# Experts' second product: high and low weight parts as one 512-column moving operand, its halves summed at the end of a block

## The chip, the cores and the metric

One core of a Trainium2 chip. The metric is the device time of one execution in microseconds (us), the median of several runs.

## The reference

A sequence of two layers over x of 2 x 2048 tokens and width D = 256: relative-position attention, then a pre-norm layer with plain attention and a mixture of experts. Only the experts concern the change:

```
h = layernorm(x, ln2_g, ln2_b).reshape(B * S, D)
topv, topi = top_k(h @ gate_w + gate_b, 2)
ew = sum(one_hot(topi, 8) * softmax(topv)[..., None], axis=1)
hid = relu(einsum('td,edf->etf', h, W1) + b1[:, None, :])      # DFF = 1024
out_e = einsum('etf,efd->etd', hid, W2) + b2[:, None, :]
moe = einsum('etd,te->td', out_e, ew)
```

The kernel computes only the two chosen experts of each token.

## The kernel before

The attentions and the routing fill the first 3790 us. Routing writes the tokens' rows, sorted by expert, to `sorted_rows`; `expert_stage` then works through NBLK = 39 blocks of BT = 256 rows, each for one expert. A block's 256 rows are BJ = 2 halves of 128, its 1024 hidden columns are FC = 8 chunks of 128. A unit u is one chunk of one block: b = u // 8, f = u % 8. There are 312 units.

Products keep their precision by parts: each operand is split into a high part and a low part (the rest) of the type fp32r, and three of the four products are taken: `PARTS = ((0, 0), (0, 1), (1, 0))`, index 0 for high and 1 for low.

The engines run side by side, each with its own program in a fixed order, tied by semaphores:

- SyncE's queue loads per block the rows xb, the first weight r1 (L2332, 1 MB), the second weight w2, already split in an earlier stage (L2336, 2 MB, three buffers; it waits for s_s, TensorE's last use of the buffer three blocks back), and b2.
- TensorE per unit, in this order: `first(u + 2)` (L2382, six matmuls of 256 columns into psH), `second(u)` (L2396, six matmuls of 256 columns, three per half j, accumulated into psY over the block's 8 units), and after the unit with f = 1 `turn(b + 1)` (L2368, four transposes of the next block's rows into psT). `second(u)` first waits for s_lo, the low part of the hidden values of unit u. Each matmul has a weight load (LDWEIGHTS, shown as PEld) of its own.
- ScalarE per unit: two activations of psH, to `whole` and to the high part `hid[:, 0]` (L2432). For f = 2 and 3 also one copy of psT to hb (L2418), which waits for `turn`, and for f = 5 and 6 yb, the bias times the row's weight (L2440).
- VectorE per unit: the low part `hid[:, 1]` (L2508), which waits for ScalarE's activations (s_r) and raises s_lo. Behind it, by f: for 0 to 2 and 7 the parts of the next first weight (L2451, L2456); for f = 3 `finish(b - 1)` (L2496), which reads the previous block's psY; for f = 4 `split_h(b + 1)` (L2464, L2466); for f = 5 `pick(b + 1)`.
- GpSimd per block: two scatter-adds of y to the output (L2353).

psY is [128, 2, BJ, 512] of fp32 in PSUM: one bank of 512 columns for each parity q of the block and each half j; before the change only 256 of the 512 columns are used.

Of the kernel before, what the change touches and what calls it, by code (L numbers as in the profile page):

```python
# [9 lines left out]
ALU = mybir.AluOpType  # L10
AX = mybir.AxisListType

P = 128
D = 256
# [10 lines left out]
FC = DFF // P  # L25
# [101 lines left out]
NP2 = 2  # L127
# [1705 lines left out]
BJ = BT // P  # L1833
# [8 lines left out]
PARTS = ((0, 0), (0, 1), (1, 0))  # L1842
# [427 lines left out]
def expert_stage(nc, A, xs, w2_parts, acc, ident, gain, b1_t, onehot, tab):  # L2270
# [8 lines left out]
    NHID = 4  # L2279
    NW2 = 3  # L2280
    NID = 4
    with ExitStack() as ctx:  # L2282
        def sb(name, shape, dt=F32):
            return ctx.enter_context(nc.sbuf_tensor("mo_" + name, shape, dt))
# [3 lines left out]
        def sem(name):  # L2288
            sems.append(ctx.enter_context(nc.semaphore("mo_" + name)))
            return sems[-1]  # L2290

        r1 = sb("w1_raw", [P, 2, CH, DFF])
        w1, w2 = sb("w1_parts", [P, 2, 2, CH, DFF], F32R), sb("w2_parts", [P, NW2, NP2, FC, D], F32R)
# [5 lines left out]
        hid = sb("hid_parts", [P, 2, NHID, BT], F32R)  # L2299
        wsel, b1sel = sb("wsel", [P, 2, BJ, NE]), sb("b1sel", [P, 2, FC, NE])  # L2300
        wt, b1 = sb("wt", [P, 2, BJ]), sb("b1", [P, 2, FC])
        ids = sb("ids", [P, NID, BJ], U32)
        yb = sb("yb", [P, 2, BJ, D])
        y = sb("y", [P, 2, BJ, D])
        psT = ctx.enter_context(nc.psum_tensor("mo_psT", [P, CH, BT], F32))
        psH = ctx.enter_context(nc.psum_tensor("mo_psH", [P, 3, G], F32))
# [6 lines left out]
        s_t, s_hT, s_hs, s_hs1 = (sem(n) for n in ("s_t", "s_hT", "s_hs", "s_hs1"))  # L2313
        s_1h, s_1l = (sem(n) for n in ("s_1h", "s_1l"))
        s_h, s_r, s_lo, s_s = (sem(n) for n in ("s_h", "s_r", "s_lo", "s_s"))
        s_pick, s_wt, s_yb, s_y = (sem(n) for n in ("s_pick", "s_wt", "s_yb", "s_y"))
        ctx.callback(clear_semaphores, nc, sems)
        blk = ctx.enter_context(nc.Block())

# [40 lines left out]
        @blk.tensor  # L2360
        def _(pe):
            def turn(b):
                pe.wait_ge(s_x[b % 3], 16 * (b // 3 + 1))
                if b >= 1:
                    pe.wait_ge(s_hT, CH * b)
                for c in range(CH):
                    for j in range(BJ):
                        last = pe.transpose(psT[:, c, j * P:(j + 1) * P], xb[:, b % 3, j, c * P:(c + 1) * P],  # L2368
                                            ident[:, :])
                last.then_inc(s_t, 1)  # L2370

            def first(u):
                b, f = u // FC, u % FC
                q = b % 2
                if f == 0:
                    pe.wait_ge(s_hs, b + 1)
                    pe.wait_ge(s_1l, CH * (b + 1))
                if u >= 3:
                    pe.wait_ge(s_r, 2 * (u - 2))
                for c in range(CH):  # L2380
                    for m, (x, z) in enumerate(PARTS):
                        last = pe.matmul(psH[:, u % 3, 0:BT], w1[:, q, x, c, f * P:(f + 1) * P], hp[:, q, z, c, :],  # L2382
                                         start=c == 0 and m == 0, stop=c == CH - 1 and m == len(PARTS) - 1)
                last.then_inc(s_h, 1)

            def second(u):
                b, f = u // FC, u % FC
                q = b % 2
                pe.wait_ge(s_lo, u + 1)
                if f == 0:  # L2390
                    pe.wait_ge(s_w2[b % NW2], 16 * (b // NW2 + 1))
                for j in range(BJ):
                    if f == 0 and b >= 2:
                        pe.wait_ge(s_y, BJ * (b - 2) + j + 1)
                    for m, (x, z) in enumerate(PARTS):
                        last = pe.matmul(psY[:, q, j, 0:D], hid[:, x, u % NHID, j * P:(j + 1) * P],  # L2396
                                         w2[:, b % NW2, z, f, :], start=f == 0 and m == 0,
                                         stop=f == FC - 1 and m == len(PARTS) - 1)
                last.then_inc(s_s, 1)

            turn(0)
            first(0)
            first(1)
            for u in range(NU):
                if u + 2 < NU:
                    first(u + 2)
                second(u)
                if u % FC == 1 and u // FC + 1 < NBLK:
                    turn(u // FC + 1)
# [33 lines left out]
        @blk.vector  # L2443
        def _(dve):
            def high_w1(b, c):
                q = b % 2
                if c == 0:
                    dve.wait_ge(s_r1[q], 16 * (b // 2 + 1))
                    if b >= 2:
                        dve.wait_ge(s_h, FC * (b - 1))  # L2450
                dve.tensor_copy(w1[:, q, 0, c, :], r1[:, q, c, :]).then_inc(s_1h, 1)  # L2451

            def low_w1(b, c):
                q = b % 2
                dve.wait_ge(s_1h, CH * b + c + 1)
                dve.tensor_tensor(out=w1[:, q, 1, c, :], in0=r1[:, q, c, :], in1=w1[:, q, 0, c, :], op=ALU.subtract  # L2456
                                  ).then_inc(s_1l, 1)

            def split_h(b):
                q = b % 2  # L2460
                dve.wait_ge(s_hT, CH * (b + 1))
                if b >= 2:
                    dve.wait_ge(s_h, FC * (b - 1))
                dve.tensor_copy(hp[:, q, 0, :, :], hb[:, q, :, :]).then_inc(s_hs1, 1)  # L2464
                dve.wait_ge(s_hs1, b + 1)
                dve.tensor_tensor(out=hp[:, q, 1, :, :], in0=hb[:, q, :, :], in1=hp[:, q, 0, :, :], op=ALU.subtract  # L2466
                                  ).then_inc(s_hs, 1)

            def pick(b):
                q = b % 2  # L2470
                dve.wait_ge(s_x[b % 3], 16 * (b // 3 + 1))
                if b >= 2:
                    dve.wait_ge(s_r, 2 * FC * (b - 1))
                    dve.wait_ge(s_yb, BJ * (b - 1))
                if b >= NID:
                    dve.wait_ge(s_sc[q], 16 * BJ * (b // 2 - 1))
                one = onehot[:, b:b + 1, :]
                dve.tensor_tensor(out=wsel[:, q, :, :], in0=xb[:, b % 3, :, EW0:EW0 + NE],
                                  in1=one.to_broadcast([P, BJ, NE]), op=ALU.mult).then_inc(s_pick, 1)
                dve.tensor_tensor(out=b1sel[:, q, :, :], in0=b1_t[:, :, :], in1=one.to_broadcast([P, FC, NE]),  # L2480
                                  op=ALU.mult).then_inc(s_pick, 1)
                dve.tensor_copy(ids[:, b % NID, :], xb[:, b % 3, :, ID0]).then_inc(s_pick, 1)
                dve.wait_ge(s_pick, 4 * b + 2)
                dve.reduce_sum(wt[:, q, :], wsel[:, q, :, :], AX.X).then_inc(s_pick, 1)
                dve.wait_ge(s_pick, 4 * b + 4)
                dve.reduce_sum(b1[:, q, :], b1sel[:, q, :, :], AX.X).then_inc(s_wt, 1)

            def finish(b):
                q = b % 2
                dve.wait_ge(s_s, FC * (b + 1))  # L2490
                dve.wait_ge(s_yb, BJ * (b + 1))
                dve.wait_ge(s_wt, b + 1)
                if b >= 2:
                    dve.wait_ge(s_sc[q], 16 * BJ * (b // 2))
                for j in range(BJ):
                    dve.scalar_tensor_tensor(out=y[:, q, j, :], in0=psY[:, q, j, 0:D], scalar=wt[:, q, j:j + 1],  # L2496
                                             in1=yb[:, q, j, :], op0=ALU.mult, op1=ALU.add).then_inc(s_y, 1)

            pick(0)
            split_h(0)  # L2500
            for c in range(CH):
                high_w1(0, c)
            for c in range(CH):
                low_w1(0, c)
            for u in range(NU):
                b, f = u // FC, u % FC
                dve.wait_ge(s_r, 2 * (u + 1))
                dve.tensor_tensor(out=hid[:, 1, u % NHID, :], in0=whole[:, u % NHID, :], in1=hid[:, 0, u % NHID, :],  # L2508
                                  op=ALU.subtract).then_inc(s_lo, 1)
                if b + 1 < NBLK:  # L2510
                    if u == 0:
                        high_w1(1, 0)
                    if f == 0:
                        low_w1(b + 1, 0)
                    if f == 1:
                        high_w1(b + 1, 1)
                    if f == 2:
                        low_w1(b + 1, 1)
                if f == 3 and b >= 1:
                    finish(b - 1)  # L2520
                if b + 1 < NBLK:
                    if f == 4:
                        split_h(b + 1)
                    if f == 5:
                        pick(b + 1)
                if f == 7 and b + 2 < NBLK:
                    high_w1(b + 2, 0)
            finish(NBLK - 1)


# [90 lines left out]
```

## Time and profile before

| | |
|---|---|
| runs, us | 4268.16, 4260.19, 4265.67 |
| median, us | 4265.67 |
| span of the profiled execution, us | 4272.5 |
| TensorE busy, us (share) | 3916.3 (92%) |
| VectorE busy, us (share) | 3446.8 (81%) |
| ScalarE busy, us (share) | 2970.6 (70%) |
| experts' stage | from about 3790 us to the end |

The span is that of one profiled execution, from its first to its last instruction; no separate time of that execution was given beside it, and it lies 6.8 us above the median of the timed runs. "PE" is TensorE's matmuls, "PEld" its weight loads, which overlap the matmuls, "DVE" VectorE, "ACT" ScalarE, "SPq" the DMA queue of SyncE. A matmul's shown duration includes its way through the pipeline, so it is longer than the distance to the next one; the distances between starts tell the pace.

### The profile page before, as it was taken

How to read it: one execution, taken by the hardware profiler on the slowest of the kernel's cores; microseconds unless marked ns; L12 is line 12 of the kernel's file. 1: busy time of each engine (PE TensorE's matmuls, PEld its weight loads, DVE VectorE, ACT ScalarE, POOL GpSimd, SP SyncE). 2: the span in 40 equal slices, each digit the busy share in tenths (PEclk: the TensorE clock that was granted, in tenths of full speed). 3: DMA queues.
4: the chain of work that ended last, by engine and by line, in shares of the span. 5: the costliest groups of instructions: out<-in, count | busy, mean ns of one | idle time of the engine just before them, and what ended most of it. 6: DMA issues, size and time to landing. Idle time of an engine off the chain costs nothing. (4 is left out here: it accounts for less than half of the span.)

```text
span 4272.5 us, 78522 instructions
## 1 busy us (share of the span) xinstructions
PE 3916.3 (92%) x26838; PEld 2067.2 (48%) x26838; DVE 3446.8 (81%) x6397; ACT 2970.6 (70%) x5963; POOL 1500.0 (35%) x1461
## 2 busy tenths in 40 slices
PE   8699999999999999996879999999999999759998
PEld 5344545545455445543533333333333333659998
DVE  7788888888888888862778889898888884657776
ACT  4077878778878777884218888888888887236666
POOL 0356666666666665652110000001010100533333
PEclk9599999999999999998969999999999999779999
DMA  8666666667677767643773333334243331679997
GB/s 315 156 162 162 163 165 168 161 163 168 163 165 168 166 161 169 167 120 108 243 155 60 64 60 64 61 56 77 47 72 56 63 53 41 160 264 325 322 326 222
DMA packets 479567, 636.81 MB, mean 149 GB/s; under 512 B 61752, under 2 KB 404520, under 8 KB 464960
## 3 DMA queue, kind: packets, MB, share of 16 engines
q1 hardware_dynamic: 460640, 608.46, 55.7%
q0 software_dynamic: 18528, 23.34, 2.9%
q8 instruction: 213, 3.49, 0.4%
q14 instruction: 186, 1.52, 0.1%
HBM read 413.78 MB, written 216.78 MB: 148 GB/s over the span
## 5 line engine op out<-in xcount | busy, mean ns | idle before, releaser
L399 DVE TENSOR_REDUCE pa_pm<-pa_psA 128x2 f32<-128x1024 f32 x1024 | 1208.3, 1219 | 133.5 <-PE pa_psA L484 133.3
L1122 ACT ACTIVATE ra_p<-ra_psS 128x512 f32<-128x512 f32 x2048 | 1082.4, 605 | 316.1 <-PE ra_psS L1199 224.2
L1033 DVE TENSOR_REDUCE ra_pm<-ra_psA 128x1 f32<-128x896 f32 x1024 | 1113.2, 1087 | 157.1 <-PE ra_psA L1157 142.2
L458 ACT ACTIVATE pa_p<-pa_psS 128x512 f32<-128x512 f32 x2048 | 1063.4, 603 | 245.9 <-PE pa_psS L510 241.7
L510 PE MATMUL pa_psS<-pa_qs,pa_zs 50*128 50x512 f32 x2048 | 792.1, 464 | 77.9 <-ACT pa_p L458 63.9
L484 PE MATMUL pa_psA<-pa_zs,pa_qs 48*128 48x512 f32 x2048 | 795.6, 471 | 38.4 <-DMA pa_zs<-k_halves 18.2
L1157 PE MATMUL ra_psA<-ra_zs,ra_qs 48*128 48x512 f32 x2048 | 730.7, 451 | 19.3 <-DVE ra_pm L1035 8.4
L1199 PE MATMUL ra_psS<-ra_qs,ra_zs 50*128 50x512 f32 (+3 forms) x2176 | 699.7, 407 | 28.9 <-ACT ra_p L1122 20.7
L510 PEld LDWEIGHTS pa_psS<-pa_qs,pa_zs 50*128 50x128 f32 x2048 | 341.6, 184 | 625.4 <-ACT pa_p L458 609.2
L1230 PE MATMUL ra_psO<-ra_p,ra_vs 128*32 128x512 f32 (+3 forms) x6400 | 552.8, 450 | 0.0
L1199 PEld LDWEIGHTS ra_psS<-ra_qs,ra_zs 50*128 50x128 f32 x2176 | 351.1, 186 | 412.1 <-ACT ra_p L1122 318.1
L521 PE MATMUL pa_psO<-pa_p,pa_vs 128*32 128x512 f32 x4096 | 546.3, 605 | 0.0
L484 PEld LDWEIGHTS pa_psA<-pa_zs,pa_qs 48*128 48x128 f32 x2048 | 346.0, 189 | 207.8 <-DVE pa_pm L399 160.0
L1157 PEld LDWEIGHTS ra_psA<-ra_zs,ra_qs 48*128 48x128 f32 x2048 | 322.6, 191 | 130.5 <-DVE ra_pm L1035 68.4
L363 POOL COPY pa_vs<-pa_vall 128x256 f32<-128x256 f32 x32 | 12.7, 398 | 1014.9 <-PE pa_psO L521 981.1
L973 POOL TENSOR_TENSOR ra_blk<-ra_blk 128x508 f32<-128x508 f32 x128 | 162.8, 1272 | 415.9 <-DMA ra_blk<-window_rows 380.1
L2382 PE MATMUL mo_psH<-mo_hp,mo_w_parts 128*128 128x256 f32 x1872 | 277.8, 285 | 5.9 <-DVE mo_w_parts L2456 5.9
L2396 PE MATMUL mo_psY<-mo_w_parts,mo_hid_parts 128*128 128x256 f32 x1872 | 273.2, 282 | 3.1 <-DVE mo_hid_parts L2508 3.1
L2353 POOL DMA_INDIRECT out<-mo_y,mo_ids x78 | 143.5, 1840 | 351.4 <-DVE mo_y L2496 331.0
L1230 PEld LDWEIGHTS ra_psO<-ra_p,ra_vs 128*32 128x32 f32 x6400 | 193.2, 109 | 121.2 <-ACT ra_p L1122 59.0
L2382 PEld LDWEIGHTS mo_psH<-mo_hp,mo_w_parts 128*128 128x128 f32 x1872 | 245.1, 190 | 6.2 <-issue 6.2
L2396 PEld LDWEIGHTS mo_psY<-mo_w_parts,mo_hid_parts 128*128 128x128 f32 x1872 | 243.6, 189 | 3.5 <-DVE mo_hid_parts L2508 3.5
(247 smaller groups left out, 4995.7 us busy)
## 6 DMA issues: line engine op xcount, KB each, us to landing
mo_w_parts<-second_weight_parts SPq DMA_DIRECT2D x39, 2048.0 KB
relative_rows<-ra_rst SPq DMA_DIRECT2D x128, 512.0 KB
ra_blk<-window_rows SPq DMA_DIRECT2D x128, 512.0 KB, 4.6
ra_zs<-k_halves SPq DMA_DIRECT2D x192, 248.0 KB, 7.6
mo_w_raw<-ffn_W SPq DMA_DIRECT2D x39, 1024.0 KB, 11.6
ra_dl<-relative_rows SPq DMA_DIRECT2D x128, 256.0 KB, 5.5
window_rows<-ra_pc SPq DMA_DIRECT2D x128, 256.0 KB, 4.4
pa_qs<-q_halves SPq DMA_DIRECT2D x192, 128.0 KB, 6.4
```

What stands on the lines that cost most here:

```text
L399: dve.reduce_max(pm[:, par, 2 * a:2 * a + 2], psA[w][:, :, :], AX.X).then_inc(s_am.h, 1)
L458: act.activation(pr[:, i % NPR, :], psS[:, slot(i), :], ACT.Exp).then_inc(s_ex.h, 1)
L484: last = pe.matmul(psA[w][:, half, :], qs[0:PR, k % U, i * P:(i + 1) * P], zs[0:PR, k % U, e * G:(e + 1) * G], start=True, stop=True)
L510: pe.matmul(psS[:, slot(i), :], zs[at:at + PR + NP2, p % U, z * P:(z + 1) * P], qs[at:at + PR + NP2, p % U, c * G:(c + 1) * G], start=True ...
L521: last = pe.matmul(psO[32 * m:32 * m + 32, :], vs[:, p % 2, 4 * (k % 4) + m, :], pr[:, (4 * k + m) % NPR, :], start=k % 4 == 0, stop=k % 4 ...
L1033: dve.reduce_max(pm[:, q, i, 2 * left:2 * left + 1], psA[w][:, lo:lo + 2 * G - P], AX.X).then_inc(s_far.h, 1)
L1122: act.activation(dst, psS[:, slot(i), :], ACT.Exp if kind == "E" else ACT.Copy).then_inc(s_cp.h, 1)
L1157: last = pe.matmul(psA[w][:, half * G:(half + 1) * G], qs[0:PR, q, i * P:(i + 1) * P], zs[0:PR, q, at:at + G], start=True, stop=True)
L1199: last = pe.matmul(dst[:, lo:hi], zs[at:at + PR + NP2, q, z * P:(z + 1) * P], qs[at:at + PR + NP2, q, c * G + lo:c * G + hi], start=True, ...
L1230: last = pe.matmul(psO[32 * m:32 * m + 32, lo:hi], v[:, z, :], pr[:, (4 * k + m) % NPR, lo:hi], start=n == 0, stop=n == 3, tile_position=( ...
L2382: last = pe.matmul(psH[:, u % 3, 0:BT], w1[:, q, x, c, f * P:(f + 1) * P], hp[:, q, z, c, :], start=c == 0 and m == 0, stop=c == CH - 1 an ...
L2396: last = pe.matmul(psY[:, q, j, 0:D], hid[:, x, u % NHID, j * P:(j + 1) * P], w2[:, b % NW2, z, f, :], start=f == 0 and m == 0, stop=f == ...
```

## The change

In `second`, the matmul of the high hidden part with the high part of the weight and the one with the low part become one: the moving operand is both parts, 2 x 256 = 512 columns, and the output is the whole bank of psY, the first 256 columns for the high part and the other 256 for the low part. The third matmul (low hidden part, high weight part) adds into the first 256 columns as before. In `finish`, the two halves are summed: a first operation per j computes yc = psY[256:512] x wt + yb, and a second y = psY[0:256] x wt + yc, which waits for the first through the new semaphore s_yc. yc is a new buffer in SBUF.

```
-        yb = sb("yb", [P, 2, BJ, D])
+        yb, yc = sb("yb", [P, 2, BJ, D]), sb("yc", [P, 2, BJ, D])
...
-                    for m, (x, z) in enumerate(PARTS):
-                        last = pe.matmul(psY[:, q, j, 0:D], hid[:, x, u % NHID, j * P:(j + 1) * P],
-                                         w2[:, b % NW2, z, f, :], start=f == 0 and m == 0,
-                                         stop=f == FC - 1 and m == len(PARTS) - 1)
+                    pe.matmul(psY[:, q, j, :].rearrange("p (z d) -> p z d", z=NP2), hid[:, 0, u % NHID, j * P:(j + 1) * P],
+                              w2[:, b % NW2, :, f, :], start=f == 0, stop=False, skip_group_check=True)
+                    last = pe.matmul(psY[:, q, j, 0:D], hid[:, 1, u % NHID, j * P:(j + 1) * P], w2[:, b % NW2, 0, f, :],
+                                     start=False, stop=f == FC - 1, skip_group_check=True)
                 last.then_inc(s_s, 1)
...
                 for j in range(BJ):
+                    dve.scalar_tensor_tensor(out=yc[:, q, j, :], in0=psY[:, q, j, D:2 * D], scalar=wt[:, q, j:j + 1],
+                                             in1=yb[:, q, j, :], op0=ALU.mult, op1=ALU.add).then_inc(s_yc, 1)
+                for j in range(BJ):
+                    dve.wait_ge(s_yc, BJ * b + j + 1)
                     dve.scalar_tensor_tensor(out=y[:, q, j, :], in0=psY[:, q, j, 0:D], scalar=wt[:, q, j:j + 1],
-                                             in1=yb[:, q, j, :], op0=ALU.mult, op1=ALU.add).then_inc(s_y, 1)
+                                             in1=yc[:, q, j, :], op0=ALU.mult, op1=ALU.add).then_inc(s_y, 1)
```

## Rows read from the trace of the kernel before

**Rows 1.** The page: the span.

```profile
span 4272.5 us, 78522 instructions
```

**Rows 2.** Busy time by stretch, instructions (x), granted clock, DMA share, GB/s.

```profile
3300.00:3400.00 100.00, 93.62 (x610) 31.61 (x608) 89.77 (x84) 81.14 (x158) 9.05 (x7) 1.00 0.35 60
...
3700.00:3800.00 100.00, 52.46 (x243) 47.06 (x243) 46.46 (x235) 20.27 (x32) 50.09 (x50) 0.61 0.62 190
...
4000.00:4100.00 100.00, 100.00 (x850) 100.00 (x849) 77.13 (x176) 67.82 (x166) 30.57 (x17) 1.00 0.96 326
```

**Rows 3.** Waits from 3800 us on: total us, times, longest.

```profile
POOL out L2353 <- DVE mo_y L2496: 331.0, 38, 49.4
...
PEld mo_psY L2396 <- DVE mo_hid_parts L2508: 3.5, 2, 3.3
...
SPq L2336 <- PE mo_psY L2396: 287.5, 36, 8.9
```

**Rows 4.** The chain that ended last: start us, us, what.

```profile
3840.27 0.72 PE mo_psH L2382 x6
...
4241.69 0.72 PE mo_psH L2382 x6
```

**Rows 5.** Timeline of the weight loads in one block: start us, us, what.

```profile
4004.85 0.47 PEld L2368 LDWEIGHTS mo_psT<-ident,mo_xb 128*128 128x128 f32 x4
...
4006.00 0.78 PEld L2396 LDWEIGHTS mo_psY<-mo_w_parts,mo_hid_parts 128*128 128x128 f32 x6
4006.71 0.78 PEld L2382 LDWEIGHTS mo_psH<-mo_hp,mo_w_parts 128*128 128x128 f32 x6
...
4008.84 0.78 PEld L2396 LDWEIGHTS mo_psY<-mo_w_parts,mo_hid_parts 128*128 128x128 f32 x6
...
4010.26 0.78 PEld L2396 LDWEIGHTS mo_psY<-mo_w_parts,mo_hid_parts 128*128 128x128 f32 x6
```

**Rows 6.** Timeline of VectorE in the same block.

```profile
4006.92 0.43 DVE L2508 TENSOR_TENSOR mo_hid_parts<-mo_hid,mo_hid_parts 128x256 fp32r<-128x256 f32 x1 [1.46 <-ACT mo_hid_parts L2432]
4007.27 0.87 DVE L2496 SCALAR_TENSOR_TENSOR mo_y<-mo_psY,mo_wt,mo_yb 128x256 f32<-128x256 f32 x2
4008.11 0.43 DVE L2508 TENSOR_TENSOR mo_hid_parts<-mo_hid,mo_hid_parts 128x256 fp32r<-128x256 f32 x1
4008.45 0.42 DVE L2464 CAST mo_hp<-mo_hb 128x512 fp32r<-128x512 f32 x1
4008.91 0.69 DVE L2466 TENSOR_TENSOR mo_hp<-mo_hb,mo_hp 128x512 fp32r<-128x512 f32 x1
4009.52 0.42 DVE L2508 TENSOR_TENSOR mo_hid_parts<-mo_hid,mo_hid_parts 128x256 fp32r<-128x256 f32 x1
...
4010.53 0.41 DVE L2508 TENSOR_TENSOR mo_hid_parts<-mo_hid,mo_hid_parts 128x256 fp32r<-128x256 f32 x1
```

**Rows 7.** Timeline of ScalarE in the same block.

```profile
4005.59 0.57 ACT L2418 ACTIVATE mo_hb<-mo_psT,gain 128x256 f32<-128x256 f32 x1 [1.73 <-PE mo_psT L2368]
...
4006.42 0.48 ACT L2432 ACTIVATE mo_hid_parts<-mo_psH,mo_b 128x256 fp32r<-128x256 f32 x1
```

**Rows 8.** Timeline of TensorE in the plain attention, 512 columns.

```profile
2503.09 0.40 PE L510 MATMUL pa_psS<-pa_qs,pa_zs 50*128 50x512 f32 x1
2503.09 0.40 PE L484 MATMUL pa_psA<-pa_zs,pa_qs 48*128 48x512 f32 x1
2503.32 0.41 PE L510 MATMUL pa_psS<-pa_qs,pa_zs 50*128 50x512 f32 x1
2503.33 0.41 PE L484 MATMUL pa_psA<-pa_zs,pa_qs 48*128 48x512 f32 x1
```

**Rows 9.** Groups by line: count, busy us, mean ns, idle before.

```profile
L2496 DVE SCALAR_TENSOR_TENSOR mo_y<-mo_psY,mo_wt,mo_yb 128x256 f32<-128x256 f32 x78 | 34.0, 477 | 1.2 <-PE mo_psY L2396 1.1
```

**Rows 10.** Timeline of the last units and the last `finish`.

```profile
4258.94 0.43 DVE L2508 TENSOR_TENSOR mo_hid_parts<-mo_hid,mo_hid_parts 128x256 fp32r<-128x256 f32 x1 [0.99 <-ACT mo_hid_parts L2432]
4259.42 0.77 PEld L2396 LDWEIGHTS mo_psY<-mo_w_parts,mo_hid_parts 128*128 128x128 f32 x6 [0.18 <-DVE mo_hid_parts L2508]
4260.43 0.88 DVE L2496 SCALAR_TENSOR_TENSOR mo_y<-mo_psY,mo_wt,mo_yb 128x256 f32<-128x256 f32 x2 [1.06 <-PE mo_psY L2396]
```

More of the change, by code:

```diff
@@ L2315, in expert_stage @@
         s_h, s_r, s_lo, s_s = (sem(n) for n in ("s_h", "s_r", "s_lo", "s_s"))
-        s_pick, s_wt, s_yb, s_y = (sem(n) for n in ("s_pick", "s_wt", "s_yb", "s_y"))
+        s_pick, s_wt, s_yb, s_yc, s_y = (sem(n) for n in ("s_pick", "s_wt", "s_yb", "s_yc", "s_y"))
         ctx.callback(clear_semaphores, nc, sems)
```

## The prediction

> **What bounds the kernel now.** I read the page first: the profiled execution spans 4272.5 us [rows 1], 6.8 us (0.16%) more than the median of the timed runs, 4265.67. The sum below is made against that span, and its difference is carried over to the median. Then the table of stretches [rows 2]: the experts' stage, where the whole change lies, runs from about 3790 us on, and there TensorE's busy time, weight loads' busy time and the DMA share are 100, 100 and 96 of 100, at a granted clock of 1.00, which is 2.4 GHz. Two candidates for the bound, so the waits decide [rows 3]: TensorE waited for VectorE 3.5 us in the whole stage and for no DMA, while the DMA queue that loads the second weights sat 287.5 us waiting for TensorE to be done with a buffer. So the order is: TensorE sets the pace, the DMA queue is paced by it, and the DMA engines have about 4% in hand. The chain that ended last says the same [rows 4]: from 3840.27 to 4241.69 it is 34 equal blocks, 401.42 / 34 = 11.806 us each.
>
> Inside a block I read the weight loads in order of time [rows 5]. Six pairs of load and matmul of the second product start at 4006.00 and the next six at 4006.71, so a pair costs 118 ns; 256 columns at 2.4 GHz are 107 ns of it. VectorE in the same stretch [rows 6] is where the little slack is. The low part for f = 3 (L2508) starts at 4006.92, then `finish` runs its two operations, then the low part for f = 4 runs 4008.11 to 4008.54, and TensorE takes it at 4008.84. What anchors this is not the matmuls of the last few units but the four transposes of `turn` at 4004.85: ScalarE's hb follows them, then its copies for f = 3, which end at 4006.90 [rows 7], and VectorE's low part starts 0.02 later.
>
> **What the change removes on TensorE.** One matmul and one weight load of each three, 624 of each over 39 blocks x 8 units x 2 halves. The columns streamed stay 768 per unit and half, so only what a pair costs beyond its columns can be saved. Before, three pairs are 3 x 118 = 354 ns. After, one pair of 512 columns and one of 256. The trace has no 128-row matmul of 512 columns of this type at full clock with a load before each; the nearest are the attention's [rows 8], where two matmuls of 512 columns follow at 2503.09 and 2503.33 (0.23 to 0.24 us apart on the two lines). By that row: 235 + 118 = 353, a saving of 1 ns, and -4 at the upper reading. By the pair's own fixed part (118 - 107 = 11 ns, the same at any width): 224 + 118 = 342, a saving of 12. If the wide pair had no fixed part at all it would be 213 + 118 = 331, a saving of 23, the bound below. I take 6 ns, between the two likelier ends: 16 per block x 6 = 0.10 us per block, 3.7 us over the stage if nothing else happened.
>
> The Trainium skill has a rule here (TensorE: Matmul & The Clock Gate, Back-to-back issue gap): isolated matmuls are spaced by their columns over 2.4 GHz plus about 2.5 ns, so three of 256 would be about 328 ns and 512 + 256 about 325. By that rule the saving would be 3 ns, inside the bounds above; the trace's 118 ns for 256 columns with a load before each [rows 5] is more than the rule's 109, so I work from the rows.
>
> **What it adds on VectorE.** Two more operations of 128x256 in each `finish`, 78 in all. The existing two take 0.87 us from start to end and one alone is 477 ns on average [rows 6, 9], so the second starts 0.87 - 0.48 = 0.39 after the first. The new wait of the first y on s_yc is for an operation that ended about 0.3 us before, since another lies between; I cost it at nothing, and at most 0.05 each. So `finish` grows by 2 x 0.39 = 0.79 us, at most 0.9. VectorE as a whole has room (77 of 100 busy [rows 2], and 0.79 / 11.8 adds 7), but `finish` is placed ahead of the low part for f = 4, for which TensorE waits.
>
> The step: the low part for f = 4 now starts at 4008.11 + 0.79 = 4008.90 and ends at 4009.33. From its end to the load that waits for it the trace shows 0.05 us (4258.94 + 0.43 to 4259.42, the one late wait of [rows 10]). The load can start at 4009.38; it would have started at 4008.84. TensorE stands 0.54 us. Behind it everything on TensorE moves by that much, since it issues in order: `first` of f = 7, the next weights' release. What is late next? On VectorE, split_h and the low part for f = 5 move by 0.79 too: from 4009.52 to 4010.31, end 4010.73, plus 0.05 is 4010.78; TensorE comes for it at 4010.26 + 0.54 = 4010.80. So it is just in time, and the later ones gain room (f = 6 starts 1.0 us after f = 5, TensorE asks 1.42 after). ScalarE isn't late: it waits for TensorE's first product, which is issued two units ahead. By the end of the block VectorE has caught up, TensorE can't, and as VectorE's place in the next block hangs on `turn`, which moved with TensorE, the stall comes back in each block.
>
> Per block: + 0.54, less the saving. Of the 16 savings, the four between `turn` and the stall (f = 2 and 3) buy nothing, since the stall's end is set by VectorE: TensorE only arrives earlier. 12 x 6 ns = 0.07. Net + 0.47 us per block. It needs a `finish` before f = 4 and a `turn` before it: blocks 1 to 37, so 37 x 0.47 = 17.4. Blocks 0 and 38 save 0.2 together. In block 38 there is no turn and ScalarE has less to do, so its low parts come earlier and I count no stall.
>
> **The end.** The last `finish` waits for the last matmul and its two operations start at 4260.43 [rows 10]; the scatters follow. The first y is written 0.79 us later: + 0.8.
>
> **The DMA side** gets easier: the same bytes per block in 12.3 instead of 11.8 us. The scatter-add's engine waited 331 us for y [rows 3], so y's 0.79 us delay lies beside idle time, apart from the end. yc costs memory only. PSUM: the 512-column write fills the bank that `finish` does not read in that block.
>
> Sum: 17.4 - 0.2 + 0.8 = + 18.0 us. The profile's span would be 4290.5, the median 4283.7.
>
> **Rivals.**
> 1. *The added VectorE work stays hidden* (not slower). It decides at 0.25 us: if the two operations delay the low part for f = 4 by less than that (0.30 of slack less 0.05 of signalling), TensorE never stands. For it: VectorE has 23% idle. Against: that idle time lies elsewhere, the low part before `finish` had idle time ahead of it because of ScalarE [rows 6], and none lies between `finish` and f = 4. Time: - 3.7 + 0.8 = - 2.9, 4263; with the largest saving (23 ns x 624 = 14.4) 4252.
> 2. *A wide matmul costs far less than two narrow ones* (faster). If weight loads and not columns set the pace, 512 columns cost like 256: 118 ns saved per unit and half, 12 x 0.118 = 1.42 per block against 0.54. Then the DMA engines would be the bound: at a share of 0.96 [rows 2] the block can shrink by 4%, 0.47 us, so 37 x 0.47 = 17.4 us less and 0.8 more at the end, 4249. Against: the attention's wide matmuls are 0.23 us apart [rows 8], and TensorE's transposes with half the columns take 109 ns (4 loads in 0.47, the last one 0.14 [rows 5]), less than the 118.
> The Trainium skill would have it so: the same section of the same page gives a sustained 131 ns for a matmul of 512 columns with its load. The rows of the attention do not bear that out.
> 3. *The stall is larger*: with 0.45 per operation and a costly s_yc wait, 0.9 + 0.1 instead of 0.79, f = 5 late by a further few hundredths, and no saving at all: 0.75 per block, + 28.6, 4294.
> 4. *The pauses lower the clock.* In 3700 to 3800 the granted clock is 0.61 with TensorE 52 of 100 busy; in 3300 to 3400 it is 1.00 with 94 busy [rows 2]. After the change TensorE is idle 0.54 of 12.3 us, 4%. At 94 busy it stayed up, so I give this 2%; a tenth of the stage at half clock would be + 44, 4328.
>
> **Chances.** Forecast (a net loss of 0.25 to 0.65 per block) 0.78; rival 1 0.10; rival 2 0.03; rival 3 0.07; rival 4 0.02. The forecast's own bounds: stall 0.54 with the full 23 ns gives 37 x (0.54 - 0.28) = 9.6 - 0.7 + 0.8 = + 9.7, 4275; 0.9 of added work with no saving, 37 x 0.65 + 0.8 = + 25, 4291. Range 4272 to 4293. About 0.2% (8.5 us) is what a measurement here can tell from no change: slower by more than that is the forecast nearly whole and rivals 3 and 4, 0.84; within 0.2% most of rival 1, and a forecast at its lower end, 0.11; faster, rival 2 and rival 1 with the large saving, 0.05.
>
> **What would show it.** In the changed profile: a new wait of the L2396 load for L2508, some 37 times, each about 0.54, 20 us in total, always the unit after `finish`; four operations in `finish` in 1.65 us; blocks of 12.28 us in the chain; 512-column matmuls 224 to 235 ns before the next start; DMA share down to about 0.93. I am wrong if that wait is missing or shorter than 0.2 us, if the block is 11.8 or less, or if a unit other than f = 4 stalls.

## The result and the profile after

The changed kernel takes 4281.49 us, median of 13 runs (4269.62 to 4293.79), beside 4268.26 us for the kernel before in its 13 runs on the same chips (4260.19 to 4278.5). The ratio is 1.0036, 95% interval 1.0025 to 1.0047: slower by 0.36%, some 15 us (the two medians alone are 13.2 apart), where +18.0 us (0.42%) was forecast.

The page of the changed kernel, span and busy time:

```profile
span 4281.9 us, 77353 instructions
...
PE 3922.3 (92%) x26214; PEld 2037.9 (48%) x26214; DVE 3479.9 (81%) x6475; ACT 2968.8 (69%) x5963; POOL 1492.5 (35%) x1461
```

Its waits from 3800 us on (who waited for whom: total us, times, longest us), and the DMA queue's own:

```profile
POOL out L2353 <- DVE mo_y L2500: 349.5, 38, 48.3
...
PEld mo_psY L2395 <- DVE mo_hid_parts L2512: 16.0, 38, 0.4
PE mo_psY L2395 <- DVE mo_hid_parts L2512: 8.3, 37, 0.2
...
SPq L2336 <- PE mo_psY L2397: 302.2, 36, 8.8
```

Against [rows 3], one wait is new: the weight load of the second product waits for the low part of the hidden values in every block, where the whole stage of before had 3.5 us of it. The view counts only idle time of the engine (a load shown as 0.19 us overlaps the next), so 0.4 here isn't the whole delay. That is read from the timeline of one block, the weight loads first (start us, us, what):

```profile
4005.34 0.47 PEld L2368 LDWEIGHTS mo_psT<-ident,mo_xb 128*128 128x128 f32 x4
...
4007.90 0.19 PEld L2395 LDWEIGHTS mo_psY<-mo_w_parts,mo_hid_parts 128*128 128x128 f32 x1
...
4009.80 0.19 PEld L2395 LDWEIGHTS mo_psY<-mo_w_parts,mo_hid_parts 128*128 128x128 f32 x1 [0.43 <-DVE mo_hid_parts L2512]
```

and VectorE in the same block:

```profile
4007.42 0.42 DVE L2512 TENSOR_TENSOR mo_hid_parts<-mo_hid,mo_hid_parts 128x256 fp32r<-128x256 f32 x1 [1.43 <-ACT mo_hid_parts L2432]
...
4007.76 0.87 DVE L2496 SCALAR_TENSOR_TENSOR mo_yc<-mo_psY,mo_wt,mo_yb 128x256 f32<-128x256 f32 x2
...
4008.55 0.87 DVE L2500 SCALAR_TENSOR_TENSOR mo_y<-mo_psY,mo_wt,mo_yc 128x256 f32<-128x256 f32 x2
...
4009.33 0.42 DVE L2512 TENSOR_TENSOR mo_hid_parts<-mo_hid,mo_hid_parts 128x256 fp32r<-128x256 f32 x1
```

`finish` occupies 4007.76 to 4009.33, 1.57 us for four operations (0.39 each). The low part for f = 4 ends at 4009.75, and the load that needs it starts at 4009.80. From the first transpose of `turn` to that load it is now 4009.80 - 4005.34 = 4.46 us; before it was 4008.84 - 4004.85 = 3.99 [rows 5]. The low part for f = 3, anchored to `turn` through ScalarE, has kept its place: 2.08 us after it, 2.07 before [rows 5, 6].

The length of a block is the distance of `turn` from block to block. The first transpose loads of two blocks that lie 33 apart, changed kernel:

```profile
3834.70 0.37 PEld L2368 LDWEIGHTS mo_psT<-ident,mo_xb 128*128 128x128 f32 x3
...
4236.93 0.37 PEld L2368 LDWEIGHTS mo_psT<-ident,mo_xb 128*128 128x128 f32 x3
```

402.23 / 33 = 12.189 us, against 11.806 [rows 4]: +0.383 per block. TensorE's matmuls in the changed kernel, in order of time:

```profile
4001.95 0.39 PE L2395 MATMUL mo_psY<-mo_w_parts,mo_hid_parts 128*128 128x512 f32 x1
...
4002.18 0.28 PE L2397 MATMUL mo_psY<-mo_w_parts,mo_hid_parts 128*128 128x256 f32 x1
...
4002.30 0.39 PE L2395 MATMUL mo_psY<-mo_w_parts,mo_hid_parts 128*128 128x512 f32 x1
...
4002.52 0.28 PE L2397 MATMUL mo_psY<-mo_w_parts,mo_hid_parts 128*128 128x256 f32 x1
...
4002.64 0.88 PE L2382 MATMUL mo_psH<-mo_hp,mo_w_parts 128*128 128x256 f32 x6
```

Wide to narrow 0.22 to 0.23 us, narrow to the next 0.12: 0.345 us for both at this place, where three narrow ones took 0.354. So the removed work did give time back, and the stall took more. The stretch 4000 to 4100 shows the stall as well: matmuls 98.23 of 100, where they were 100 before, VectorE 81.50, and the clock still 1.00. Weight loads are at 91.22, in part because there are fewer of them:

```profile
4000.00:4100.00 100.00, 98.23 (x691) 91.22 (x691) 81.50 (x188) 66.39 (x164) 29.91 (x17) 1.00 0.96 317
```

From the first transpose of the stage to the end, the changed kernel takes 4281.9 - 3780.03 = 501.9 us; its row is

```profile
3780.03 0.50 PEld L2368 LDWEIGHTS mo_psT<-ident,mo_xb 128*128 128x128 f32 x3 [27.68 <-DMA mo_xb<-sorted_rows]
```

and the kernel before

```profile
3785.29 0.50 PEld L2368 LDWEIGHTS mo_psT<-ident,mo_xb 128*128 128x128 f32 x3 [26.88 <-DMA mo_xb<-sorted_rows]
```

so 4272.5 - 3785.3 = 487.2 us. The stage grew by 14.7 us. The two spans differ by only 9.4, because the stage happened to begin 5.3 us sooner, with nothing changed ahead of it. The stage's own length leaves that out, and I use it and the block's length beside the ratios below. The stage has some scatter of its own at its start: from its first transpose to the `turn` of the third block it took 30.65 us before and 30.29 in the changed kernel, 30.3 to 30.7 in nine of the ten traces of this document, and 27.84 in the tenth (that of the last experiment). The block's length is the steadiest of the three.

### The profile page after: what moved, and what is told of

It reads as the page before. It is cut to its first block and busy times, and to the rows that moved or that the text cites. A ratio compares the mean times of both kernels' runs of the same rounds, so it can differ in the third digit from the quotient of the medians.

```text
span 4281.9 us, 77353 instructions
## 1 busy us (share of the span) xinstructions
PE 3922.3 (92%) x26214; PEld 2037.9 (48%) x26214; DVE 3479.9 (81%) x6475; ACT 2968.8 (69%) x5963; POOL 1492.5 (35%) x1461
## 5 line engine op out<-in xcount | busy, mean ns | idle before, releaser
L484 PE MATMUL pa_psA<-pa_zs,pa_qs 48*128 48x512 f32 x2048 | 795.9, 471 | 38.3 <-DMA pa_zs<-k_halves 18.2
L2395 PE MATMUL mo_psY<-mo_w_parts,mo_hid_parts 128*128 128x512 f32 x624 | 235.0, 398 | 11.7 <-DVE mo_hid_parts L2512 11.7
L1128 ACT ACTIVATE ra_sw<-ra_sw,ra_nm 128x256 f32<-128x256 f32 x512 | 243.6, 529 | 0.0
```

The source lines that it names most:

```text
L484: last = pe.matmul(psA[w][:, half, :], qs[0:PR, k % U, i * P:(i + 1) * P], zs[0:PR, k % U, e * G:(e + 1) * G], start=True, stop=True)
L2395: pe.matmul(psY[:, q, j, :].rearrange("p (z d) -> p z d", z=NP2), hid[:, 0, u % NHID, j * P:(j + 1) * P], w2[:, b % NW2, :, f, :], start=f ...
```

## The experiments

The first four ran together on one chip, the last four on another; each group is compared with runs of the kernel before on the same chip (medians 4262.59 and 4273.69 us). Of the account to be tested, two parts can be separated: longer VectorE work in `finish`, and the wide matmul.

**VectorE's part alone.** Six narrow matmuls as before; in `finish`:

```
+                for j in range(BJ):
+                    dve.scalar_tensor_tensor(out=yc[:, q, j, :], in0=psY[:, q, j, 0:D], scalar=wt[:, q, j:j + 1],
+                                             in1=yb[:, q, j, :], op0=ALU.mult, op1=ALU.add).then_inc(s_yc, 1)
                 for j in range(BJ):
+                    dve.wait_ge(s_yc, BJ * b + j + 1)
                     (y as before)
```

> VectorE's part alone: the kernel before with its six narrow matmuls, but finish does four operations as in the changed kernel. The two added ones write yc from the same PSUM columns and nothing reads yc; the output is as before. My account (VectorE's longer finish makes the low part for f = 4 late): TensorE stands 0.54 us per block in 37 blocks, block 11.81 -> about 12.33 us (the changed kernel has 12.19), +20 us over the kernel before, ratio about 1.005. Rival (the wide matmul itself is the cause, its 512 columns being slow or delaying the readers): block 11.81 and a ratio of 1.000.

Measured: 4279.55 us, ratio 1.0039 (1.0026 to 1.0052). `turn` of two blocks 33 apart:

```profile
3823.52 0.36 PEld L2368 LDWEIGHTS mo_psT<-ident,mo_xb 128*128 128x128 f32 x3
...
4228.22 0.36 PEld L2368 LDWEIGHTS mo_psT<-ident,mo_xb 128*128 128x128 f32 x3
```

12.264 us per block, +0.457. The stall stands at the same unit, in its trace as

```profile
3995.21 0.47 PEld L2368 LDWEIGHTS mo_psT<-ident,mo_xb 128*128 128x128 f32 x4
...
3999.66 0.42 PEld L2396 LDWEIGHTS mo_psY<-mo_w_parts,mo_hid_parts 128*128 128x128 f32 x3 [0.39 <-DVE mo_hid_parts L2512]
```

4.45 us after `turn` (3.99 before, 4.46 in the changed kernel). The slowdown is VectorE's and doesn't need the wide matmul; the rival falls. The stall is 0.46 and not the 0.54 that I expected, the time +17 us and not +20.

**The wide matmul alone.** TensorE as changed; `finish` as before (shown against the changed kernel), with two operations on columns 0 to 255, so the product of high hidden and low weight part is missing from the output.

```
-                for j in range(BJ):
-                    dve.scalar_tensor_tensor(out=yc[:, q, j, :], in0=psY[:, q, j, D:2 * D], ...)
-                for j in range(BJ):
-                    dve.wait_ge(s_yc, BJ * b + j + 1)
                     dve.scalar_tensor_tensor(out=y[:, q, j, :], in0=psY[:, q, j, 0:D], scalar=wt[:, q, j:j + 1],
-                                             in1=yc[:, q, j, :], ...)
+                                             in1=yb[:, q, j, :], ...)
```

> The wide matmul alone: TensorE as in the changed kernel, finish as in the kernel before. The sum of the upper 256 columns is left out, so the product of the high hidden part and the low weight part is missing from the output. My account: no stall at f = 4, and each wide and narrow matmul together save 6 to 11 ns against three narrow ones, 0.10 to 0.18 us per block: block 11.63 to 11.71 us, -4 to -7 us over the kernel before, ratio 0.998 to 0.999. Rival (wide matmul the cause): block 12.2 us as in the changed kernel. Second rival (the DMA engines are the bound as soon as TensorE is faster): block stays at 11.8 and new waits for DMA appear.

Measured: 4261.67 us, ratio 0.9998 (0.9987 to 1.001). `turn`, 33 blocks apart:

```profile
3826.00 0.37 PEld L2368 LDWEIGHTS mo_psT<-ident,mo_xb 128*128 128x128 f32 x3
...
4212.09 0.37 PEld L2368 LDWEIGHTS mo_psT<-ident,mo_xb 128*128 128x128 f32 x3
```

11.700 us per block, -0.107, that is 6.7 ns for each of 16 wide-and-narrow pairs. The stretch view shows a TensorE that never stands and DMA engines that keep up, at 0.97 (third column from the right is the clock, then the share):

```profile
4000.00:4100.00 100.00, 100.00 (x719) 94.41 (x719) 77.23 (x178) 69.73 (x173) 27.99 (x18) 1.00 0.97 331
```

So the wide matmul costs nothing by itself. The kernel's time, 0.9 us under before where 4 to 7 were expected, doesn't show the gain. Its stage is 482.8 us, 4.4 less than before: 0.1% of the kernel, less than the interval of the ratio, which therefore neither shows nor denies it; the block's length shows it.

**The same work in another place.** The changed kernel, yc still behind f = 3, y behind f = 5, pick behind f = 6:

```
                     if f == 4:
                         split_h(b + 1)
-                    if f == 5:
+                if f == 5 and b >= 1:
+                    finish_y(b - 1)
+                if b + 1 < NBLK:
+                    if f == 6:
                         pick(b + 1)
```

`finish` keeps only the two yc operations; `finish_y` has the two y operations and the wait for the scatter that last read y. After the last unit both run.

> The changed kernel with finish taken apart: the two yc operations stay behind the low part for f = 3, the two y operations go behind the low part for f = 5, and pick, which overwrites the weights that finish reads, goes behind the low part for f = 6. No place has more than 0.8 us added. My account (what costs is where the VectorE work stands, not how much it is): no wait of TensorE for VectorE but a few hundredths, block 11.63 to 11.75 us, ratio to the kernel before 0.998 to 1.000, to the changed kernel about 0.996. Rival (VectorE has too little room in a block for 0.79 us more, wherever it stands): the stall moves to another unit and the block stays near 12.2.

Measured: 4262.75 us, ratio to before 0.9995 (0.9985 to 1.0006). Block 11.700 us, exactly that of the wide matmul alone, and no wait of TensorE for VectorE among the waits of the blocks. All four VectorE operations are there, so it was not their amount in a block that cost, but that they stood together ahead of one item with little slack. Yet the stage is 4264.5 - 3778.9 = 485.6 us, only 1.6 shorter than before where the blocks give 4. The rest is at the end, from the last `turn` on: 33.84 us, where the kernel before takes 31.46. GpSimd's last scatter-adds of this kernel show it:

```profile
4249.28 1.56 POOL L2353 DMA_INDIRECT out<-mo_y,mo_ids  x1 [0.30 <-issue]
4253.64 1.56 POOL L2353 DMA_INDIRECT out<-mo_y,mo_ids  x1 [2.79 <-DMA out<-mo_y,mo_ids]
```

The last block's scatter waits 2.79 us for the landing of the block before it, whose y now comes two units later.

**The new order without the change.** The kernel before with `finish` behind f = 5 and pick behind f = 6.

```
-                if f == 3 and b >= 1:
+                if f == 5 and b >= 1:
                     finish(b - 1)
...
-                    if f == 5:
+                    if f == 6:
                         pick(b + 1)
```

> The kernel before with its finish of two operations behind the low part for f = 5 and pick behind f = 6: the new order without the change. TensorE never waited at f = 4, so my account expects nothing: block 11.81, ratio 1.000 within 0.001. If this order alone is faster, what e3 gains is not the wide matmul's.

Measured: 4264.1 us, ratio 1.0002 (0.9991 to 1.0012), block 11.807 us, stage 489.8 us: nothing in the blocks, and 2.6 us more at the end, again with the last scatter waiting for the DMA (3.01 us). So the 0.107 per block of the kernel above is the wide matmul's.

**The end mended.** As the third, with finish_y behind f = 3 in the last block:

```
-                if f == 5 and b >= 1:
+                if f == (5 if b + 1 < NBLK else 3) and b >= 1:
                     finish_y(b - 1)
```

> As e3_spread, but in the last block the y operations of the block before stand behind f = 3 again, so that the last scatter-adds need not wait for those before them. Reason: in e3's trace the last scatter waited 2.79 us for the DMA of the scatters before it, where the kernel before waited for y; e3's blocks are 11.70 us, but its stage only 1.6 us shorter. My account: block 11.70 as in e3, 4 us gained in the stage and 0.8 given back by the last finish, -3 us against the kernel before, ratio 0.999; the wait of the last scatter is for y. Rival (the end is long for another reason): ratio as e3, 0.9995, and the wait for the DMA is still there.

Measured: 4274.0 us (12 runs, 4263.42 to 4301.99) beside 4273.69, ratio 1.0006 (0.9991 to 1.0021): undecided. Its trace does what was expected. GpSimd's last scatter waits for y again:

```profile
4252.48 1.56 POOL L2353 DMA_INDIRECT out<-mo_y,mo_ids  x1 [0.30 <-issue]
4257.38 1.56 POOL L2353 DMA_INDIRECT out<-mo_y,mo_ids  x1 [3.34 <-DVE mo_y L2503]
```

the block is 11.700 us, and the stage 4268.1 - 3784.4 = 483.7 us, 3.5 less than before and 18.2 less than the changed kernel. A gain of 3.5 us (0.08%) over before is below what these runs can tell. This version is clear of the changed kernel's loss. That it beats the kernel before is shown for the length of a block and seen in the stage of one profiled execution; for the kernel's time it isn't shown.

**One added operation instead of two.** The kernel before with one operation more in each `finish` (yc for j = 0, unused):

```
+                for j in [0, 1][:1] * 1:
+                    dve.scalar_tensor_tensor(out=yc[:, q, j, :], in0=psY[:, q, j, 0:D], ...)
                 for j in range(BJ):
                     (y as before)
```

> The kernel before with one added VectorE operation per finish instead of two (it writes yc, which nothing reads; the output is as before). My account with a threshold: finish could let the low part for f = 4 start 0.06 us earlier than ScalarE allows, and 0.25 us more pass before TensorE waits, so of 0.39 us 0.08 remain: block 11.89 us, +3 us. Rival (cost in proportion to the added work, half of e1's 0.46 per block): block 12.04 us, +8.5 us.

Measured: 4275.45 us, ratio 1.0009 (0.9998 to 1.0019). `turn`, 33 blocks apart:

```profile
3851.66 0.36 PEld L2368 LDWEIGHTS mo_psT<-ident,mo_xb 128*128 128x128 f32 x3
...
4243.97 0.36 PEld L2368 LDWEIGHTS mo_psT<-ident,mo_xb 128*128 128x128 f32 x3
```

11.888 us per block, +0.082 (0.08 expected, 0.23 if the cost were in proportion). The ratio's interval includes 1, so it is the block that decides here.

**Four added operations.** The same with four (results unused):

```
+                for j in range(2 * BJ):
+                    dve.scalar_tensor_tensor(out=yc[:, q, j, :], in0=psY[:, q, j % 2, 0:D], ...)
```

> The kernel before with four added VectorE operations per finish (results that nothing reads; the output is as before). Threshold account: 4 x 0.395 = 1.58 us less 0.31 is 1.27 us per block, block 13.08 us, 37 x 1.27 + 1.6 at the end = +49 us, ratio 1.011. Proportional account (0.23 per operation): block 12.73 us, +36 us.

Measured: 4320.93 us, ratio 1.0103 (1.0088 to 1.0118). `turn`, 33 blocks apart:

```profile
3850.15 0.36 PEld L2368 LDWEIGHTS mo_psT<-ident,mo_xb 128*128 128x128 f32 x3
...
4280.98 0.36 PEld L2368 LDWEIGHTS mo_psT<-ident,mo_xb 128*128 128x128 f32 x3
```

13.055 us per block, +1.249, and +47 us for the kernel (+49 expected, +36 if the cost were in proportion). The four kernels with narrow matmuls lie on one line with a threshold: 0, 1, 2 and 4 added operations cost 0, 0.082, 0.457 and 1.249 us; from one to two it is 0.375 and from two to four 0.396 for each, close to an operation's full 0.39, and it starts at 0.31 to 0.33 us of added work.

**All four operations behind f = 5.** The changed kernel, `finish` behind f = 5 (f = 3 in the last block), pick behind f = 6:

```
-                if f == 3 and b >= 1:
+                if f == (5 if b + 1 < NBLK else 3) and b >= 1:
                     finish(b - 1)
```

> The changed kernel with all four operations of finish behind the low part for f = 5 (f = 3 in the last block) and pick behind f = 6. At f = 5 the low part starts about 5.0 us after the transposes; four operations of 0.395 later the one for f = 6 starts, ends 7.02 us after them and is seen at 7.07, where TensorE asks at 6.79: a stall of 0.28 us at f = 6, block 11.98 us, +7 us over the kernel before, ratio 1.0015. Rival (the place behind f = 3 alone is short of time): block 11.70.

Measured: 4279.46 us, ratio 1.0014 (1.0004 to 1.0025), block 11.975 us (11.98 expected), and the stall has moved to f = 6, two units after the one of the changed kernel:

```profile
4002.91 0.19 PEld L2395 LDWEIGHTS mo_psY<-mo_w_parts,mo_hid_parts 128*128 128x128 f32 x1 [0.19 <-DVE mo_hid_parts L2512]
```

The `turn` of that block stands at 3995.86, so this load comes 7.05 us after it, where 7.07 was expected. So the place behind f = 3 has nothing special but its slack: the same reckoning, made at another unit, gives that unit's stall.

## Why the prediction held, step by step

- **The bound.** TensorE sets the pace and the DMA queue is paced by it: shown. With TensorE faster by 0.107 us per block TensorE waited for no DMA.
- **The saving on TensorE.** Taken as 6 ns per pair of a wide and a narrow matmul, measured 6.7 over a block. From the starts of all matmuls in 30 blocks, a wide one in the second experiment is followed after 228 ns in the mean (224 to 230 mostly) and a narrow one after 118. So the prediction's two readings, 224 and 235, were bounds on either side; the fixed part is about 15 ns at 512 columns and 12 at 256, not the same at both as one of its readings had it. By these starts a pair saves 8.5 ns, 0.136 us over 16 pairs. The six matmuls of the first product, whose edit is none, take 0.03 us more per block than before, which leaves the 0.107; why they do is open. The attention's rows [rows 8] weren't a like case: there two matmuls of 50 and 48 rows start at the same time, so in them 0.235 us passes for two wide matmuls, and they spoke less against the second rival than the prediction took them to.
- **The added VectorE work.** 2 x 0.39 us: right, four operations take 1.57 us. The wait on s_yc costs nothing that shows: with it operations start 0.393 us apart, and in the kernel with four added ones, which has no such wait, 0.392.
- **The stall.** The mechanism, the unit and the count (TensorE waited 37 times) are right; its size is the term that was mis-sized, 0.54 for 0.46 to 0.47. The step that failed is "the low part for f = 4 now starts at 4008.11 + 0.79", with the reading under the first rival that no idle time lies between `finish` and that low part. In the kernel before, the start at 4008.11 was not set by VectorE, which was free at 4007.27 + 2 x 0.39 = 4008.05, but by ScalarE's copy for f = 4, which ended at 4008.08:

```profile
4007.58 0.50 ACT L2432 ACTIVATE mo_hid_parts<-mo_psH,mo_b 128x256 fp32r<-128x256 f32 x1
```

These 0.06 us were slack too. In the changed kernel the low part starts 3.99 us after `turn` and not 3.26 as before, 0.73 later and not 0.79; the threshold is 0.31 and not 0.25, as one and four added operations show.
- **What is late next.** Nothing, as forecast: f = 5 was just in time, later units not late, and the stall comes back in each block.
- **Savings inside the stall's shadow.** Four of 16 were said to buy nothing. The changed kernel's +0.383 against +0.457 for VectorE's part alone leaves 0.074 of the 0.107, so 11 of 16, where 12 were forecast. Right within a pair.
- **The end.** + 0.8: the last y starts at 4269.72 behind yc at 4268.93, 0.79 later than with two operations.

```profile
4268.93 0.88 DVE L2496 SCALAR_TENSOR_TENSOR mo_yc<-mo_psY,mo_wt,mo_yb 128x256 f32<-128x256 f32 x2 [1.07 <-PE mo_psY L2397]
4269.72 0.87 DVE L2500 SCALAR_TENSOR_TENSOR mo_y<-mo_psY,mo_wt,mo_yc 128x256 f32<-128x256 f32 x2
```

- **The sum.** 37 x 0.383 = 14.2, + 0.8 = 15.0, and 14.7 in the stage, for 18.0 forecast; the missing 3 are the 0.08 of the stall, 37 times. That 15.0 and 14.7 lie so close is in part luck, since the start of the stage was 0.36 us shorter in the changed kernel's trace.
- **The signs.** The new wait is there in every block, but the view shows about 0.42 us of it each time and 16.0 in total, not 0.54 and 20. The DMA share was to fall to about 0.93; in the stretch 4000 to 4100 it stayed at 0.96, and only the rate fell, from 326 to 317 GB/s. Why the share doesn't follow the rate wasn't tried; nothing in the sum rests on it.
- **The rivals.** Hidden VectorE work: wrong where the change put it, true for another order (the third experiment). A wide matmul at the price of a narrow one: 0.228 us between starts against 0.118, so no. That is also the measurement on the Trainium skill's sustained 131 ns for 512 columns (TensorE: Matmul & The Clock Gate, Back-to-back issue gap): here it is 228 ns, nearer to the 216 that the same section gives for an isolated one. The clock: 1.00 in the stage with TensorE's pauses, so no.

## What to carry to other kernels

When work is added to an engine that has idle time in total, look up the next thing that another engine waits for in its program, and measure how long that thing may be late: here 0.31 us out of a block of 11.8, while nearly a quarter of the engine's time was idle. Added work costs only what it exceeds that slack by, and beyond it each operation costs its full length in every round. Dividing the same operations between two places, each with slack enough, gave the time back here; moving all four of them behind another item moved the stall there, with 0.27 us of it left. When reading the slack, check also whether the start of the late instruction was set by its own engine or by another one, since that difference belongs to the slack; and follow a moved result to the program's end, where it may delay the last transfers.

## What was not expected of the hardware

- A matmul of 128 x 128 with a weight load of its own costs about 12 ns beyond its columns at full clock when it is 256 wide (118 ns to the next start) and about 15 when it is 512 wide (228 ns), in the mean over 30 blocks of the second experiment. So merging two into one saved only 8.5 ns where it was done.
- The stage ahead of the experts' isn't steady from run to run: in ten profiled executions, with the same code up to there, the first transpose of this stage came between 3768.6 and 3797.2 us after the start, while the blocks of the kernel before are 11.80 to 11.81 us long each. Differences under 0.2% in this kernel's total are better read from the stage's own rows, the length of its blocks above all.
